# A decoder layer on one core: the row maxima of three batch pairs are added in PSUM by TensorE instead of by VectorE on the way to SBUF

## The chip, the core and the metric

The kernel runs on one core of one Trainium2 chip. The metric is the device time of one execution in microseconds; lower is better. The kernel before has a median of 912.19 us over 3 runs (910.69 to 912.86). The chip's instruction engines are TensorE (PE in the profile), VectorE (DVE), ScalarE (ACT), GpSimd (POOL) and SyncE (SP), each with a queue of its own that it works off in order. SyncE only issues DMAs here.

## The reference

One decoder layer on x of shape 16 x 128 x 256 in float32:

```
x = layernorm(x + attention(x))        # 16 heads of 16, full softmax over 128 keys, output projection
x = layernorm(x + recurrence(x, ctx))  # a running state per channel, exponentials of k = x, values v = ctx
x = layernorm(x + experts(x))          # 8 experts, 256 -> 1024 -> 256 with gelu, softmax gates
```

For the change only the softmax of the attention matters:

```
scores = softmax(einsum('bhse,bhte->bhst', q, k) * scale, axis=-1)
att    = einsum('bhst,bhte->bhse', scores, v)
```

In the experts each takes the best 128 of 128 tokens, that is all of them, so every token passes through every expert with its gate as weight.

## The kernel before, in words

**Pairs.** The 16 batches are worked in 8 pairs (p = 0 to 7) of 256 tokens. For each pair there is a chain of steps: X (transpose), QK and V (projections), S_0 to S_3 (scores), M_0 to M_3 (row maxima and shift), E_0 to E_3 (exponentials), T_0 to T_3 (transposes of the probabilities), W_0 to W_3 (products with the values and their sums), ATT, WO, NORM1, Y1, XEXP, REC_0 to REC_3 (the recurrence), BACK, NORM2 and the router's steps R_TURN to R_BIAS. A step name stands for its parts on all engines: S on TensorE, M on VectorE, E on ScalarE, T and W on several.

**Units.** Each of the four units u of a pair holds 8 heads of one batch in two groups of 4 heads, 128 x 512 numbers each, so a pair has 8 groups (QUADS). Scores of a group stand in half-banks of PSUM (`score_banks`, L464, and `half`, L475). Pair 0's unit 1 uses the tensors up_ps and down_ps; pair 1's units 0 and 1 use a part of down_ps, which the experts' down products write later.

**Softmax, two ways** (`direct`, L381, true for p < DIRECT = 1). For pair 0, VectorE takes negated row maxima (L1246) and ScalarE reads the scores in PSUM head by head, 32 activations of 128 x 128 with the maximum as bias (L1022). For all other pairs VectorE takes the maxima (L1246), then adds them to the scores on the way into the SBUF tensor probs (the shift, L1255), and ScalarE takes exponentials there, 8 activations of 128 x 512 (L1028). `shifted` counts the shifts, `probs_ready` the exponentials, `max_ready` the maxima. The probabilities of pairs 0 and 1 are transposed by TensorE (L699) and copied by ScalarE (pt_hi, L1041) and VectorE (pt_lo, L1266); from pair 2 on they are split into p_hi (ScalarE, L1034) and p_lo (VectorE, L1261) and transposed by DMA. W is TensorE's L722 and L723 and VectorE's L1272 to L1276, which ends in att.

**Experts.** A visit n is one pass of an expert's weights; pair p joins at visit JOIN[p] = 0, 5, 9, ... for 8 visits, so one or two pairs are in work at a time. A visit has 4 units (one pair) or 8 (two pairs); U(n, u) is the up product (L629 to L631; L905 to L909 for the very first), D(n, u) the down product (L932 to L934). ScalarE applies gelu (h_all, L1087) and rounds to h_hi (L1078), VectorE takes the rest h_lo (L1167). Weights come by DMA as raw pieces, which ScalarE rounds to w_hi (L1100) and VectorE completes to w_lo (L1167; GpSimd, L1494, for the first ones). At the end of a visit VectorE adds the down products with their gates (acc, L1377).

**What sets the order.** `plan` (L57) makes one line of items: U(0,0), U(0,1), U(0,2), U(0,3), U(1,0), D(0,0), D(0,1), U(1,1), D(0,2), U(1,2), D(0,3), U(1,3), U(2,0), D(1,0), D(1,1), U(2,1), D(1,2), U(2,2), ... with the numbers 0, 1, 2, ... Each engine goes through this line. The tables EARLY (pairs 1 and 2) and STEADY (the others) say behind which item each step of a pair stands; in pair 2's part item 39 is U(5,1), 40 D(4,2), 49 U(5,6), 51 U(5,7), 54 D(5,5), 56 D(5,6), 57 U(6,2), 61 D(6,0). Pair 0's steps and some of pair 1 to 3 stand ahead of the line in lists per engine (FIRST_PE, FIRST_ACT, FIRST_DVE, FIRST_POOL, L1571 to L1581). Within an item ScalarE takes h_hi and gelu first, then the steps outside of BY_TABLE, the weight splits, and last the steps of BY_TABLE (E_0 to E_3, XEXP, R_GATE), which need another activation table than gelu (L1137 to L1160). VectorE takes acc, h_lo, the steps, then the weight splits. On SyncE nothing of the order is touched.

TensorE's D(0,0) waits for the weights and for h_lo alone:

```
pe.wait_ge(h_ready, unit + 1)
pairs = len(active(n))
if n == 1 and u == 0:
    pe.wait_ge(x2_biased, 1)
```

## Time and profile before

| | |
|---|---|
| median of 3 runs | 912.19 us |
| lowest, highest | 910.69, 912.86 us |
| profiled execution, its own time | 912.31 us |
| its span | 910.5 us |
| mean granted TensorE clock | 0.984 |
| busy: TensorE | 872.2 us (96%) |
| busy: VectorE | 586.0 us (64%) |
| busy: ScalarE | 579.8 us (64%) |
| busy: GpSimd | 80.7 us (9%) |
| chain that ended last | TensorE 76%, ScalarE 9%, VectorE 5% |

How to read it: the profile is of one execution. Busy time counts what an engine executes, not the waiting or the issue of DMAs. The times of a timeline row are its start and its length in microseconds; "x8" says that eight instructions in a row are merged; a bracket at the end is the idle time of the engine ahead of the row and what ended it. Instructions on one engine overlap a little, so a row's length divided by its count is slightly above the distance from one to the next. PEclk is the granted TensorE clock as a share of 2.4 GHz; 0.50 is 1.2 GHz.

### The profile page before, as it was taken

How to read it: one execution, taken by the hardware profiler on the slowest of the kernel's cores; microseconds unless marked ns; L12 is line 12 of the kernel's file. 1: busy time of each engine (PE TensorE's matmuls, PEld its weight loads, DVE VectorE, ACT ScalarE, POOL GpSimd, SP SyncE). 2: the span in 40 equal slices, each digit the busy share in tenths (PEclk: the TensorE clock that was granted, in tenths of full speed). 3: DMA queues.
4: the chain of work that ended last, by engine and by line, in shares of the span. 5: the costliest groups of instructions: out<-in, count | busy, mean ns of one | idle time of the engine just before them, and what ended most of it. 6: DMA issues, size and time to landing. Idle time of an engine off the chain costs nothing.

```text
span 910.5 us, 17548 instructions
## 1 busy us (share of the span) xinstructions
PE 872.2 (96%) x6507; PEld 794.6 (87%) x6507; DVE 586.0 (64%) x1197; ACT 579.8 (64%) x975; POOL 80.7 (9%) x116
## 2 busy tenths in 40 slices
PE   7898878989999999999999999999999999999997
PEld 7788777879998998988988898889988888999997
DVE  6889698767766567656566675655675564333574
ACT  7688677766666555766557465665557665444683
POOL 4220012001200012000120010100120000000000
PEclk8899889999999999999999999999999999999999
DMA  8469998998849653785539854496537855655340
GB/s 265 153 228 340 367 320 297 290 305 274 276 132 240 221 186 127 192 250 188 166 109 240 236 184 150 133 238 220 175 125 194 246 187 163 193 187 176 96 139 12
DMA packets 196787, 187.09 MB, mean 205 GB/s; under 512 B 62024, under 2 KB 162144, under 8 KB 196704
## 3 DMA queue, kind: packets, MB, share of 16 engines
q1 hardware_dynamic: 196704, 185.98, 67.5%
q8 instruction: 53, 0.87, 0.4%
q14 instruction: 30, 0.25, 0.1%
HBM read 136.91 MB, written 36.44 MB: 190 GB/s over the span
## 4 chain that ended last, share of the span: by engine, by line
PE 76%; ACT 9%; DVE 5%; DMA 2%; issue 2%; SPq 1%; POOL 1%; POOLq 0%; ACTq 0%; DVEq 0%
PE down_ps L932 12%; PE down_ps L933 11%; PE down_ps L934 11%; PE up_ps L629 11%; PE up_ps L631 11%; PE up_ps L630 11%; DMA pt_lo<-p_lo 2%; ACT h_all L1087 2%; ACT probs L1028 1%; PE bank L651 1%; PE bank L676 1%; ACT L1087 1%; PE bank L629 1%; PE bank L630 1%; PE bank L631 1%
## 5 line engine op out<-in xcount | busy, mean ns | idle before, releaser
L1087 ACT ACTIVATE h_all<-up_ps,b_all 128x512 f32<-128x512 f32 (+1 forms) x296 | 182.2, 630 | 256.0 <-PE up_ps L631 245.4
L932 PE MATMUL down_ps<-w_hi,h_hi 128*128 128x256 f32 x1024 | 295.0, 288 | 4.4 <-DVE acc L1377 4.4
L1167 DVE TENSOR_TENSOR h_lo<-h_all,h_hi 128x512 fp32r<-128x512 f32 x256 | 176.0, 690 | 188.7 <-ACT h_hi L1078 188.0
L933 PE MATMUL down_ps<-w_lo,h_hi 128*128 128x256 f32 x1024 | 290.4, 284 | 0.0
L934 PE MATMUL down_ps<-w_hi,h_lo 128*128 128x256 f32 x1024 | 290.3, 283 | 0.0
L629 PE MATMUL up_ps<-x2t_hi,w_hi 128*128 128x512 f32 (+1 forms) x588 | 220.5, 375 | 2.7 <-DVE w_lo L1167 1.2
L631 PE MATMUL up_ps<-x2t_hi,w_lo 128*128 128x512 f32 (+1 forms) x588 | 215.7, 367 | 0.0
L630 PE MATMUL up_ps<-x2t_lo,w_hi 128*128 128x512 f32 (+1 forms) x588 | 215.0, 366 | 0.0
L932 PEld LDWEIGHTS down_ps<-w_hi,h_hi 128*128 128x128 f32 x1024 | 195.6, 191 | 13.0 <-issue 2.9
L933 PEld LDWEIGHTS down_ps<-w_lo,h_hi 128*128 128x128 f32 x1024 | 196.4, 192 | 7.0
L934 PEld LDWEIGHTS down_ps<-w_hi,h_lo 128*128 128x128 f32 x1024 | 196.4, 192 | 0.0
L1078 ACT ACTIVATE h_hi<-h_all 128x512 fp32r<-128x512 f32 x256 | 161.4, 631 | 33.5 <-PE down_ps L934 29.2
L631 PEld LDWEIGHTS up_ps<-x2t_hi,w_lo 128*128 128x128 f32 x588 | 111.3, 189 | 18.6
L629 PEld LDWEIGHTS up_ps<-x2t_hi,w_hi 128*128 128x128 f32 x588 | 112.4, 191 | 16.2 <-DVE w_lo L1167 1.4
L630 PEld LDWEIGHTS up_ps<-x2t_lo,w_hi 128*128 128x128 f32 x588 | 112.6, 191 | 10.5
L1167 DVE TENSOR_TENSOR w_lo<-w_raw,w_hi 128x512 fp32r<-128x512 f32 x89 | 60.9, 689 | 26.8 <-ACT w_hi L1100 26.8
L1461 POOL TENSOR_TENSOR var_eps<-moments,eps_row 128x2 f32<-128x2 f32 x24 | 7.9, 329 | 782.5 <-DVE moments L1177 782.5
L1100 ACT ACTIVATE w_hi<-w_raw 128x512 fp32r<-128x512 f32 x96 | 59.4, 628 | 0.0
L1377 DVE SCALAR_TENSOR_TENSOR acc<-down_ps,gate,acc 128x256 f32<-128x256 f32 x112 | 46.9, 475 | 3.1 <-PE down_ps L934 3.1
L1261 DVE TENSOR_TENSOR p_lo<-probs,p_hi 128x1024 f16<-128x1024 f32 x24 | 29.4, 1224 | 25.7 <-ACT p_hi L1034 25.7
L1246 DVE TENSOR_REDUCE neg_max<-bank 128x4 f32<-128x512 f32 x60 | 38.4, 680 | 4.8 <-PE bank L676 4.7
L1087 ACT ACT_TABLE_LOAD x27 | 34.6, 1283 | 0.5
(251 smaller groups left out, 948.8 us busy)
## 6 DMA issues: line engine op xcount, KB each, us to landing
w_hi<-w_parts SPq DMA_DIRECT2D x200, 256.0 KB, 3.3
w_lo<-w_parts SPq DMA_DIRECT2D x200, 256.0 KB, 3.6
w_raw<-in_w_dram SPq DMA_DIRECT2D x96, 256.0 KB, 4.3
w_parts<-w_hi SPq DMA_DIRECT2D x64, 256.0 KB, 4.1
w_parts<-w_lo SPq DMA_DIRECT2D x64, 256.0 KB, 4.6
x_in<-in_x_dram SPq DMA_DIRECT2D x8, 256.0 KB, 4.2
ctx_sb<-in_ctx_dram SPq DMA_DIRECT2D x8, 256.0 KB, 4.4
out_dram<-acc SPq DMA_DIRECT2D x8, 256.0 KB, 2.2
```

Source lines behind the costliest of these rows:

```text
L629: nc.tensor.matmul(ps, hi, rhs_hi, start=first, stop=False)
L630: nc.tensor.matmul(ps, hi, rhs_lo, start=False, stop=False)
L631: return nc.tensor.matmul(ps, lo, rhs_hi, start=False, stop=last)
L932: nc.tensor.matmul(ps, hi, w2h[:, c, :], start=c == 0 and j == 0, stop=False, skip_group_check=True)
L933: nc.tensor.matmul(ps, hi, w2l[:, c, :], start=False, stop=False, skip_group_check=True)
L934: mm = nc.tensor.matmul(ps, lo, w2h[:, c, :], start=False, stop=c == FC - 1 and j == PAIR - 1, skip_group_check=True)
L1078: nc.scalar.activation(h_hi[:, unit % HALF, :], h_all[:, unit % HALL, :], ACT.Copy).then_inc(h_hi_ready, 1)
L1087: a = nc.scalar.activation(h_all[:, unit % HALL, k * wide:(k + 1) * wide], up_ps[unit % 2][:, k * wide:(k + 1) * wide], ACT.Gelu_apprx_tan ...
L1100: nc.scalar.activation(piece((w1_hi, w2_hi)[i], i, q), raw(m, i), ACT.Copy)\
L1167: return nc.vector.tensor_tensor(dst, src, hi.bitcast(F32), ALU.subtract)
L1246: nc.vector.tensor_reduce(neg_max[:, g, :].rearrange("p (b a) -> p b a", b=2), by_tile_head(score_banks(p, u)[i], half(p, u)), AX_X, ALU.m ...
L1377: nc.vector.scalar_tensor_tensor(out=acc[:, p % 2, t, :], in0=by_tile(down_ps[down_banks(n)[a]])[:, t, :], scalar=gate[:, p % 3, t, n % E: ...
```

## The change

DIRECT becomes 3: pairs 0, 1 and 2 take the direct way, and that way is new. TensorE adds the negated maxima to the scores in PSUM: a product of the identity (a rounded copy, ident_r, made once by ScalarE) with neg_max repeated 128 times per head, two products of 256 columns for each group, 16 for each pair (`level`). ScalarE then takes one exponential of 128 x 512 for each group out of PSUM, without a bias. The 16 shifts of pairs 1 and 2 on VectorE fall away. The steps LEVEL_0 to LEVEL_2 get places on TensorE; pair 0's lists are reordered; pair 2's W_0 and W_1 move from items 54 and 55 to 56 and 57; D(0,0) gets a wait for pair 1's first four exponentials; waits on `shifted` become waits on `probs_ready` for these pairs. The scores of a second half-bank no longer start with a cleared bank. Pairs 3 to 7 stay as they are.

```diff
+        ident_r = sb("ident_r", [P, P], F32R)
...
-        neg_max = sb("neg_max", [P, QUADS, HQ])
+        neg_max = sb("neg_max", [P, QUADS, HQ], F32R)
...
+        def level_units(p, s):
+
+            if first(p):
+                return ((0,), (1,), (2, 3))[s - LEVEL_0]
+            return ((0, 1), (), (2, 3))[s - LEVEL_0]
+
+        def levelled(p, u, i):
+
+            if first(p) and u < 2:
+                return 2 * u + i + 1
+            return 4 * (u // 2) + 2 * i + 2
...
                 if u == 2 and by_dma(p):
-                    pe.wait_ge(shifted, QUADS * (p - DIRECT) + 4)
+                    if direct(p):
+                        pe.wait_ge(probs_ready, QUADS * p + 4)
+                    else:
+                        pe.wait_ge(shifted, QUADS * (p - DIRECT) + 4)
...
-                                              kd[at, k, c, :, rows], start=last == 0, stop=last == 2)
+                                              kd[at, k, c, :, rows], start=last == 0 and not (direct(p) and half(p, u)),
+                                              stop=last == 2, skip_group_check=direct(p))
...
+            def level(p, s):
+
+                taken = level_units(p, s)
+                for i in range(2):
+                    for u in taken:
+                        g = 2 * u + i
+                        pe.wait_ge(max_ready, QUADS * p + 2 * taken[-1] + i + 1)
+                        for b in range(2):
+                            mm = nc.tensor.matmul(by_tile_head(score_banks(p, u)[i], half(p, u))[:, b], ident_r[:],
+                                                  neg_max[:, g, 2 * b:2 * b + 2].rearrange("p (a o) -> p a o", o=1).to_broadcast([P, 2, S]),
+                                                  start=False, stop=True, skip_group_check=True)
+                        mm.then_inc(level_ps, 1)
...
                 if by_dma(p):
-                    if u == 0:
+                    if u == 0 and direct(p):
+                        pe.wait_ge(probs_ready, QUADS * (p + 1))
+                    if u == 0 and not direct(p):
                         pe.wait_ge(shifted, QUADS * (p - DIRECT + 1))
...
                 pairs = len(active(n))
+                if n == 0 and u == 0:
+                    pe.wait_ge(probs_ready, QUADS + 4)
...
             pe.wait_ge(masks_made, MASKS)
+            pe.wait_ge(ident_ready, 1)
...
                             g = 2 * u + i
-                            act.wait_ge(max_ready, QUADS * p + g + (1 if u % 2 or first(p) and u == 0 else 3))
-                            if u >= 2:
+                            act.wait_ge(level_ps, QUADS * p + levelled(p, u, i))
+                            if u >= 2 and by_dma(p):
+                                act.wait_ge(p_lo_ready, turns(p) + u - 1)
+                            if u >= 2 and not by_dma(p):
                                 act.wait_ge(pt_ps, QUADS * p + (g - 3))
-                            for h in range(HQ):
-                                a = nc.scalar.activation(probs[:, u % 2, i, h, :], by_tile_head(score_banks(p, u)[i], half(p, u))[:, h // 2, h % 2],
-                                                         ACT.Exp, bias=neg_max[:, g, h:h + 1])
-                            a.then_inc(probs_ready, 1)
+                            nc.scalar.activation(probs[:, u % 2, i].rearrange("p (b a) t -> p b a t", b=2),
+                                                 by_tile_head(score_banks(p, u)[i], half(p, u)), ACT.Exp).then_inc(probs_ready, 1)
...
+            act.wait_ge(masks_made, 4)
+            nc.scalar.activation(ident_r[:], ident[:], ACT.Copy).then_inc(ident_ready, 1)
             split_projection(PROJECTIONS[0])
...
-    {E_0: 3, E_1: 3, X_BIAS: 6, T_0: 7, T_1: 8, W_0: 10, W_1: 11, S_2: 13, M_2: 13, S_3: 13, M_3: 13, E_2: 15, E_3: 15, T_2: 17, T_3: 18, W_2: 20, W_3: 21,
+    {LEVEL_0: 1, E_0: 3, E_1: 3, X_BIAS: 6, T_0: 7, T_1: 8, W_0: 10, W_1: 11, S_2: 13, M_2: 13, S_3: 13, M_3: 13, LEVEL_2: 14, E_2: 15, E_3: 15, T_2: 17, T_3: 18, W_2: 20, W_3: 21,
...
-     S_0: 38, M_0: 38, S_1: 38, M_1: 38, DIAG_1: 40, E_0: 41, E_1: 41, T_0: 43, T_1: 45, S_2: 49, M_2: 49, S_3: 49, M_3: 50, W_0: 54, E_2: 54, E_3: 54, W_1: 55, T_2: 56,
+     S_0: 38, M_0: 38, S_1: 38, M_1: 38, LEVEL_0: 39, DIAG_1: 40, E_0: 41, E_1: 41, T_0: 43, T_1: 45, S_2: 49, M_2: 49, S_3: 49, M_3: 50, LEVEL_2: 51, E_2: 54, E_3: 54, W_0: 56, W_1: 57, T_2: 56,
...
-FIRST_PE = ([(0, s) for s in (X, QK, V, S_0, S_1, S_2, S_3, T_0, T_1, W_0, T_2, W_1, T_3, W_2)]
+FIRST_PE = ([(0, s) for s in (X, QK, V, S_0, S_1, LEVEL_0, LEVEL_1, S_2, S_3, T_0, T_1, LEVEL_2, W_0, W_1, T_2, T_3, W_2)]
...
-FIRST_ACT = ([(0, s) for s in (K_COPY, V, E_0, E_1, T_0, E_2, T_1, E_3, T_2, T_3)]
+FIRST_ACT = ([(0, s) for s in (K_COPY, V, E_0, E_1, T_0, T_1, E_2, E_3, T_2, T_3)]
...
-DIRECT = 1
+DIRECT = 3
```

## Rows read from the trace of the kernel before

**Rows 1.** Busy time of the engines in three stages (stretch, length, engines, PEclk, DMA share, GB/s).

```profile
16.00:33.00 17.00, 12.47 (x132) 11.19 (x132) 11.85 (x26) 13.61 (x41) 9.28 (x9) 0.70 0.64 196
...
82.00:105.00 23.00, 17.62 (x181) 16.71 (x182) 20.34 (x39) 16.45 (x31) 0.00 (x0) 0.95 1.05 368
...
190.00:910.00 720.00, 710.58 (x5170) 645.32 (x5168) 431.45 (x883) 437.82 (x692) 48.50 (x70) 1.00 0.63 185
```

**Rows 2.** Instructions that write or read probs (duration ns min/median/max, first and last start).

```profile
L1028 ACT ACTIVATE probs<-probs x56: 612/615/633, 64.3 to 706.5; 128x512 f32<-128x512 f32 x56
L1255 DVE TENSOR_TENSOR probs<-bank,neg_max x54: 675/678/682, 55.5 to 701.6; 128x512 f32<-128x512 f32 x54
```

**Rows 3.** Timeline of ScalarE, pair 0's exponentials and what follows them (start us, us).

```profile
15.40 2.09 ACT L1022 ACTIVATE probs<-bank,neg_max 128x128 f32<-128x128 f32 x8
...
19.40 1.13 ACT L1100 ACTIVATE w_hi<-w_raw 128x512 fp32r<-128x512 f32 x2
...
27.00 1.23 ACT L1041 ACTIVATE pt_hi<-up_ps 128x512 f16<-128x512 f32 x2
```

**Rows 4.** Timeline of TensorE, pair 0: S_2, T_0 and ATT.

```profile
17.63 0.80 PE L676 MATMUL bank<-kd,q_hi 32*128 32x256 f32 x8 [2.87 <-ACT probs L1022]
...
19.55 1.97 PE L699 MATMUL down_ps<-ident,probs 128*128 128x128 f32 x8 [0.26 <-ACT probs L1022]
...
33.31 0.66 PE L651 MATMUL bank<-ident,att 128*128 128x128 f32 x4 [0.17 <-DVE att L1276]
```

**Rows 5.** Timeline of TensorE: first product of U(1,0), first two of D(0,0).

```profile
61.99 0.38 PE L629 MATMUL up_ps<-x2t_hi,w_hi 128*128 128x256 f32 x1 [1.18 <-DVE w_lo L1167]
...
63.50 0.28 PE L932 MATMUL down_ps<-w_hi,h_hi 128*128 128x256 f32 x1
63.62 0.28 PE L933 MATMUL down_ps<-w_lo,h_hi 128*128 128x256 f32 x1
```

**Rows 6.** Timeline of ScalarE: pair 1's E_0 and E_1 and what follows.

```profile
64.33 2.18 ACT L1028 ACTIVATE probs<-probs 128x512 f32<-128x512 f32 x4
66.41 0.62 ACT L1078 ACTIVATE h_hi<-h_all 128x512 fp32r<-128x512 f32 x1
```

**Rows 7.** Timeline of TensorE: pair 1's S_2, U(2,1) and ATT.

```profile
82.49 0.51 PE L676 MATMUL bank<-kd,q_hi 32*128 32x256 f32 x8 [1.37 <-DVE att L1276]
...
84.93 0.28 PE L629 MATMUL up_ps<-x2t_hi,w_hi 128*128 128x256 f32 x1
...
104.76 1.12 PE L651 MATMUL bank<-ident,att 128*128 128x128 f32 x4 [4.00 <-DVE att L1276]
```

**Rows 8.** Waits of TensorE over the whole span (total us, times, longest us).

```profile
PE down_ps L864 <- ACT gate_t L1071: 1.0, 1, 1.0
```

**Rows 9.** Timeline of VectorE: pair 1's M_2 with its shifts, and pt_lo of T_2.

```profile
84.67 1.28 DVE L1246 TENSOR_REDUCE neg_max<-bank 128x4 f32<-128x512 f32 x2
85.87 1.28 DVE L1255 TENSOR_TENSOR probs<-bank,neg_max 128x512 f32<-128x512 f32 x2
...
95.12 1.29 DVE L1266 TENSOR_TENSOR pt_lo<-bank,pt_hi 128x512 f16<-128x512 f32 x2 [1.87 <-ACT pt_hi L1041]
```

**Rows 10.** Busy time behind the wait for pair 1's ATT (columns as in rows 1).

```profile
106.00:108.00 2.00, 2.00 (x11) 2.00 (x10) 0.77 (x2) 1.63 (x3) 0.00 (x0) 0.50 1.07 395
...
110.00:112.00 2.00, 2.00 (x19) 2.00 (x18) 1.04 (x3) 1.73 (x4) 0.00 (x0) 1.00 1.08 375
```

**Rows 11.** Timeline of TensorE in pair 2's part: D(4,2) and D(6,0).

```profile
146.73 0.28 PE L932 MATMUL down_ps<-w_hi,h_hi 128*128 128x256 f32 x1
...
186.21 0.36 PE L932 MATMUL down_ps<-w_hi,h_hi 128*128 128x256 f32 x1 [2.02 <-DVE acc L1377]
```

**Rows 12.** Timeline of VectorE in pair 2's part: M_1 and W_0.

```profile
147.77 1.28 DVE L1246 TENSOR_REDUCE neg_max<-bank 128x4 f32<-128x512 f32 x2
...
174.46 0.58 DVE L1272 TENSOR_REDUCE pv_sum<-bank 128x136 f32<-128x408 f32 x1
```

**Rows 13.** Timeline of ScalarE: pair 2's E_2 and E_3.

```profile
175.13 2.19 ACT L1028 ACTIVATE probs<-probs 128x512 f32<-128x512 f32 x4
```

More of the change, by code:

```diff
@@ L305, in decoder_layer @@
         max_ready = sem("max_ready")
+        ident_ready = sem("ident_ready")
+        level_ps = sem("level_ps")
         shifted = sem("shifted")
@@ L764, in attend @@
                     go_ahead(p, s)
+                if s in (LEVEL_0, LEVEL_1, LEVEL_2):
+                    level(p, s)
                 if s == X:
@@ L851, in route @@
                 if part == 4:
-                    if second(b):
+                    if second(b) and direct(b + 1):
+                        pe.wait_ge(probs_ready, QUADS * (b + 1) + 4)
+                    if second(b) and not direct(b + 1):
                         pe.wait_ge(shifted, QUADS * (b + 1 - DIRECT) + 4)
@@ L1256, in attend @@
                                                     by_tile_head(score_banks(p, u)[i], half(p, u)),
-                                                    neg_max[:, g, :].rearrange("p (b a o) -> p b a o", b=2, o=1).to_broadcast([P, 2, 2, S]),
+                                                    neg_max[:, g, :].bitcast(F32).rearrange("p (b a o) -> p b a o", b=2, o=1).to_broadcast([P, 2, 2, S]),
                                                     ALU.add).then_inc(shifted, 1)
@@ L1534 @@
  ATT, CTX, WO, NORM1, Y1, XEXP, REC_0, REC_1, REC_2, REC_3, BACK, NORM2,
- R_TURN, R_LOGITS, R_MAX, R_GATE, R_GATE_T, R_BIAS, K_LOW_1, Q_LOW_1, HEAD_X, HEAD_K_0, HEAD_K, HEAD_Q, HEAD_V) = range(58)
+ R_TURN, R_LOGITS, R_MAX, R_GATE, R_GATE_T, R_BIAS, K_LOW_1, Q_LOW_1, HEAD_X, HEAD_K_0, HEAD_K, HEAD_Q, HEAD_V, LEVEL_0, LEVEL_1, LEVEL_2) = range(61)
 DIAGONAL = (DIAG_0, DIAG_1)
```

## The prediction, made before any run of the changed kernel

> **What bounds the kernel now.** I read the stages first. From 190 us on, TensorE is busy 710.58 of 720 us; before that it is not: 12.47 of 17 us while pair 0's attention runs, 17.62 of 23 us in pair 1's second half [rows 1]. So up to 190 us a microsecond is set by the order of four in-order queues and can be won or lost; behind it TensorE alone counts, and nothing there can take a delay back. The change lies wholly in the first part: pair 0 at 14 to 33 us, pair 1 at 54 to 105, pair 2 at 145 to 190. The prices come from the group rows: a shift on VectorE lasts 0.68 us, an exponential of 512 columns 0.615 us [rows 2]. The timelines of those three places give the order, and I walk them step by step. Every wait of TensorE named below is the idle time in brackets at the end of its row. All sums are made against the profiled execution, 912.31 us (span 910.5); the median of the runs shown is 912.19, 0.12 less.
>
> **Pair 0: fewer, wider exponentials.** 32 exponentials of 128 columns become 8 of 512. The first sixteen run from 15.40 to 19.40, 0.25 us each in a row; the other sixteen stand at 22 and 25 us and end where pt_hi starts, at 27.00 [rows 3]. A wide one in a row takes 0.52: four stand between 64.33 and 66.41 [rows 6]. ScalarE so saves 16 x 0.25 - 4 x 0.52 = 1.9 us in each half. The Trainium skill, page "ScalarE: Activation LUTs", section "What ACT_TABLE_LOAD costs", prices an activation with a bias pointer at 280 ns + 0.833 ns per column, one without at 186 ns, with 93 ns of overlap; by that a half would save 2.6 us. The rows decide for 1.9.
> Against it stand the level products: TensorE may add only after VectorE's maximum (0.68 us each), and ScalarE reads only after that. In the first half the last maximum ends at 16.7, its products at about 17.15, the last exponential at 17.75 instead of 19.45. TensorE's S_2 starts at about 16.95 instead of 17.63 and T_0 at 18.35 instead of 19.55 [rows 4], since its array runs slowly there. T_0 and T_1 take 3.5 us, LEVEL_2 1.7 at that rate (8 x 0.21), so level 2 is in at 22.9 and 23.75 and the exponentials end at 25.45 instead of 27.2. VectorE, whose turn now comes without the 1.7 us gap before T_1, ends its last value sums at about 30.9 instead of 33.2, where ATT starts at 33.31 [rows 4]. From there everything up to 53 us hangs on that chain: **-2.3 us** (bounds -1.2, if the levels wait longer at the slow rate, and -4.0, the full 2 x 1.9, if the clock holds). The copy of the identity on ScalarE lies in 2.5 us in which ScalarE waits for the first weights: nothing; without that cover it costs one activation, 0.3.
>
> **Pair 1, first half: the new wait ahead of D(0,0).** LEVEL_0 goes behind U(0,1): 8 products of 256 columns. The nearest row is a product of 256 columns of the same type, one every 0.12 us (63.50, 63.62) [rows 5]: 1.0 us with the refill; at half rate it is 0.21, 1.7 us. I take 0.12. The maxima are ready by then, because four shifts less stand between them. U(0,2) and U(0,3) come 1.0 us later, but TensorE's wait of 1.18 us for w_lo at 61.99 [rows 5] goes, as VectorE reaches that split 2 us sooner. U(1,0) then ends at about 63.1, level with before.
> Now the wait that counts. D(0,0) starts at 63.50 [rows 5]. With the change it waits for pair 1's first four exponentials, because they read down_ps, which D(0,0) overwrites. Those stand in ScalarE's queue at item 3, behind two activations, a weight split, a table load and the router's exponential, and end at 66.41 [rows 6]; with U(0,3) late, at 67.1. TensorE stands from 63.1 to 67.2, **4.0 us**, and D(0,0), D(0,1), U(1,1), T_0 and all behind them stand with it. It had such a gap before ATT, at 104.76 [rows 7], and behind it the granted clock is 0.50, half of 2.4 GHz, at 106 to 108 us, and 1.00 only from 110 [rows 10]: 24 products cost 0.21 instead of 0.12, so 2.1 us more. (The Trainium skill, "TensorE: Matmul & The Clock Gate", section "Why this matters for your kernels", warns that a pause between bursts of matmuls brings the half rate back. The trace agrees with 0.50, and it speaks against this wait.) So TensorE is 3.7 + 2.1 = 5.8 late at U(1,1). It gets back what it used to wait: 1.0 for gate_t [rows 8], 1.37 for att at 82.49 [rows 7], and 0.8 in shorter gaps. VectorE's late value sums and D(1,0) both give S_2 at about 85.15: +2.65 us.
>
> **Pair 1, second half: LEVEL_2 holds U(2,1).** In the kernel before, U(2,1) starts at 84.93 straight behind D(1,1), while VectorE alternates maxima and shifts from 84.67 to 89.5 [rows 7, 9]. Now LEVEL_2 stands between them and waits for the third and fourth maximum. VectorE comes to M_2 at 87.5 (h_lo of the late U(2,0) first); four maxima of 0.6 end at 89.95, the products at 90.45, U(2,1) starts at 90.5: **+5.6 us**. Without any delay ahead it would still be 84.67 + 2.4 + 0.5 = 87.6, +2.7. Behind it hangs a closed chain: gelu of U(2,1), table load, four exponentials, h_hi, table load, gelu, T_2's pt_hi, and from 95.12 [rows 9] VectorE without a gap to att at 104.7. T_2 on TensorE now waits for all four exponentials, but ScalarE's queue is later than that. The 4 x 0.6 us that VectorE saves here end in the wait ahead of 95.12: they are worth nothing. Pair 1 in all: **+5.6**.
>
> **Pair 2.** LEVEL_0 stands behind U(5,1), where D(4,2) starts at 146.73 [rows 11]. The third and fourth maximum, at 147.77 before [rows 12], move to 146.57 and end at 147.25 and 147.8; products to 148.4: **+1.7**. The gate chain (gelu, table load, exponentials, h_hi, h_lo, acc) is ScalarE's, so VectorE's 2.4 us don't shorten it. LEVEL_2 behind U(5,7) finds its maxima nearly ready: +1.0. W_0 and W_1 move behind items 56 and 57, and W_0 now waits for all exponentials, 175.13 to 177.3 [rows 13], late by 1.0: 178.4. VectorE's two value sums, 1.1 us each, leave an empty stretch at 174.46 [rows 12] and stand now ahead of p_lo T_2 and T_3, and so ahead of acc, for which D(6,0) waits 2.02 us at 186.21 [rows 11]. By my walk acc comes at 188.6, D(6,0) at 188.8: **+2.6** with LEVEL_2's 1.0.
> DMA queues: no transfer is added. They are full at 82 to 105 us (share 1.05) [rows 1], so an earlier start gives them nothing to collide with that a later pair 1 would not relieve.
>
> **Sum.** -2.3 + 5.6 + 1.7 + 2.6 = +7.6: 912.31 + 7.6 = 919.9, less 0.12: **919.8 us**. The wide exponential from PSUM has no row: the same from SBUF lasts 0.615 [rows 2], two copies of 512 columns from PSUM 1.23 [rows 3]; both say the same, so 0.52 in a row stands, within 0.1 us over pair 1's eight. Lower end: pair 0 at -4.0, no slow clock (5.6 becomes 3.5), moved W at nothing (2.6 becomes 1.0): +2.2, 914.4. Upper end: pair 0 at -1.2, and the slow clock once more at D(6,0): 3.6 us of idle there against 2.0 before; 24 products, +2.1: 923.0.
>
> **Rivals.**
> (a) The clock holds at D(0,0), as it did over the 2.02 us at 186.21 [rows 11]: +5.5, 917.7. Against it: the clock behind 104.76 [rows 10].
> (b) The clock falls a second time at D(6,0): +9.7, 921.9. For it: idle nearer 4.0 than 2.0. Against: a walk through four queues tends to add up waits.
> (c) Only the level waits cost: D(0,0)'s 3.7 us vanish in the later waits of pair 1 and the moved W are free. -2.3 + 2.7 + 1.7 + 1.0 = +3.1, 915.3; with the clock held in pair 0 (-4.0), 913.5.
> (d) Faster: VectorE's queue sets the way to ATT, and each shift that goes shortens it. Place: the gapless stretch up to 104.7. It decides if U(2,1) starts no later than before, so that pt_lo T_2 is pulled forward by the 2.4 us. Then -2.3 - 2.4 + 1.9 (pair 2's 16 products at 0.12) = -2.8, 909.4. Against it: the 1.87 us in which VectorE waits for pt_hi ahead of 95.12 [rows 9].
>
> **Chances.** About 0.2% (1.8 us) either way can't be told from no change: 910.4 to 914.0. Forecast 0.35, (a) 0.15, (b) 0.15, (c) 0.20, of which 0.05 lies within 0.2%, (d) 0.15, of which 0.12 is faster and 0.03 within. Slower 0.35 + 0.15 + 0.15 + 0.15 = 0.80, same 0.08, faster 0.12. Range 913.5 to 923.5: it holds the forecast, (a), (b) and nearly all of (c), and leaves out (d).
>
> **What would show it.** Right: a wait of D(0,0) for probs of 3 to 4 us near 61 to 65 us (all is 2.3 earlier there) and a granted clock of 0.5 behind it; a wait of 1.5 to 2.5 us of the level products for neg_max before U(2,1); ATT of pair 0 near 31 and of pair 1 near 108; D(6,0) waiting 3 us or more for acc. Wrong: ATT of pair 1 before 104.8, or a stage behind pair 2 that is shorter or longer than its 720 us.

## Result and the profile after

The changed kernel takes 917.57 us (median of 5 executions, 913.14 to 918.40), the kernel before, run beside it, 912.32 (5, 910.69 to 914.82): ratio **1.0052**, 95% interval 1.0032 to 1.0072, slower by 4.7 us. The forecast was 919.8 in 913.5 to 923.5. The profiled execution is the lowest of the five, 913.14 us (span 911.4, mean granted clock 0.993); the other four took 917.55 to 918.40 at 0.985 to 0.988. So a second profile of the same kernel, of 915.63 us, is read beside it (the first experiment). That one too is the lowest of its round (the other five took 916.26 to 918.25); no profile shows an execution of the usual length.

Busy time of the changed kernel by stages, columns as in [rows 1]:

```profile
16.00:33.00 17.00, 14.11 (x167) 11.96 (x168) 15.53 (x31) 11.64 (x23) 9.92 (x10) 1.00 0.60 194
63.00:65.00 2.00, 1.98 (x10) 2.00 (x11) 0.69 (x1) 1.97 (x3) 0.00 (x0) 0.56 0.61 180
...
105.00:107.00 2.00, 1.21 (x11) 1.21 (x12) 1.27 (x4) 0.51 (x2) 0.00 (x0) 1.00 1.05 392
107.00:109.00 2.00, 2.00 (x20) 2.00 (x19) 1.38 (x2) 1.74 (x5) 0.00 (x0) 1.00 1.04 339
...
135.00:145.00 10.00, 7.92 (x72) 7.01 (x71) 8.25 (x18) 4.71 (x9) 5.54 (x4) 1.00 1.06 382
190.00:910.00 720.00, 712.20 (x5194) 646.81 (x5192) 432.67 (x885) 438.00 (x693) 48.53 (x70) 1.00 0.63 185
```

The clock no longer falls in pair 0 (0.70 before), it falls to 0.56 behind 63 us, and it does not fall at 105 to 109 us, where the kernel before has 0.50 [rows 10]. From 190 to 910 us TensorE is busy 712.20 us instead of 710.58 at a clock of 1.00: in this profile that part only lies later. Now TensorE's timeline, to be laid beside [rows 4, 5, 7, 11]:

```profile
15.90 0.51 PE L695 MATMUL bank<-kd,q_hi 32*128 32x256 f32 x8
...
29.27 0.66 PE L666 MATMUL bank<-ident,att 128*128 128x128 f32 x4 [0.28 <-DVE att L1320]
...
63.02 0.35 PE L973 MATMUL down_ps<-w_hi,h_hi 128*128 128x256 f32 x1 [3.97 <-ACT probs L1065]
...
80.99 0.51 PE L695 MATMUL bank<-kd,q_hi 32*128 32x256 f32 x8
...
84.93 1.31 PE L709 MATMUL bank<-neg_max,ident_r 128*128 128x256 f32 x8 [1.33 <-DVE neg_max L1290]
86.08 0.28 PE L644 MATMUL up_ps<-x2t_hi,w_hi 128*128 128x256 f32 x1
...
105.79 0.66 PE L666 MATMUL bank<-ident,att 128*128 128x128 f32 x4 [3.22 <-DVE att L1320]
...
147.31 0.28 PE L973 MATMUL down_ps<-w_hi,h_hi 128*128 128x256 f32 x1
...
187.77 0.35 PE L973 MATMUL down_ps<-w_hi,h_hi 128*128 128x256 f32 x1 [3.50 <-DVE acc L1421]
```

ATT of pair 0 comes at 29.27 instead of 33.31, and pair 1 turns these 4 us into a loss: D(0,0) waits 3.97 us for the exponentials, the level products 1.33 us for the maxima, and ATT of pair 1 is at 105.79 instead of 104.76. D(6,0) waits 3.50 us for acc instead of 2.02. Of the signs that the prediction named, the waits of D(0,0) and D(6,0) and the clock behind D(0,0) came as said. The level products wait 1.33 us ahead of U(2,1), a little under the 1.5 to 2.5 named; ATT of pair 0 is near 29 and not 31, ATT of pair 1 near 106 and not 108. ScalarE's and VectorE's rows of pair 1's second half, to be laid beside [rows 9]:

```profile
90.37 2.06 ACT L1065 ACTIVATE probs<-bank 128x512 f32<-128x512 f32 x4
```

```profile
83.00 2.48 DVE L1290 TENSOR_REDUCE neg_max<-bank 128x4 fp32r<-128x512 f32 x4
...
96.14 1.29 DVE L1310 TENSOR_TENSOR pt_lo<-bank,pt_hi 128x512 f16<-128x512 f32 x2 [1.86 <-ACT pt_hi L1083]
```

VectorE is done with the maxima at 85.5 and has no shifts, and waits 1.86 us ahead of pt_lo, as it did before (1.87). VectorE's rows ahead of D(6,0), to be laid beside [rows 12]: the first rows of the two value sums, then the addition that D(6,0) waits for.

```profile
181.16 0.58 DVE L1316 TENSOR_REDUCE pv_sum<-bank 128x136 f32<-128x408 f32 x1
...
183.96 0.58 DVE L1316 TENSOR_REDUCE pv_sum<-bank 128x136 f32<-128x408 f32 x1
...
186.75 0.87 DVE L1421 SCALAR_TENSOR_TENSOR acc<-down_ps,gate,acc 128x256 f32<-128x256 f32 x2
```

In the kernel before, the sums stood at 174.46 and 176.22, with 2.51 us of idle time of VectorE behind them. Now they stand among the splits that lead to acc, and VectorE has no gap from 179.95 to acc.

The table holds the steps of every profile as distances between starts of timeline rows (us), so that a shift in one part does not hide another. The last column names stretches of which the granted clock spent a good part at half: **p** 15 to 33 us (pair 0), **a** 61 to 69 us, **b** 100 to 111, **c** 131 to 146 (behind BACK of pair 1), **d** 171 to 195 (behind the waits of W_0 or D(6,0) in pair 2). Three more are left out of it: a fall at 120 to 135 us, behind the wait for mix, is in all but the last three rows (where it reaches past 131 us it is not counted as c); one at 92 to 98 us is in after_again, pairs01, w_back and fill_all; one at 153 to 162 us is in before, pair0, pair0_narrow, pair1_first and pairs01.

| kernel | S_0 to BACK, pair 0 | BACK 0 to S_2 of pair 1 | S_2 to ATT | ATT to BACK 1 | BACK 1 to S_0 of pair 2 | S_0 to S_2 | S_2 to end | half |
|---|---|---|---|---|---|---|---|---|
| before | 34.84 | 34.09 | 22.27 | 23.10 | 16.46 | 21.27 | 744.9 | p, b |
| after | 32.24 | 36.65 | 24.80 | 20.92 | 16.46 | 21.73 | 746.5 | a |
| after_again | 32.08 | 36.60 | 24.77 | 20.89 | 18.60 | 21.71 | 747.4 | a, c, d |
| pair0 | 33.05 | 34.09 | 22.28 | 22.45 | 16.46 | 21.27 | 744.5 | p, b |
| pair0_narrow | 32.15 | 34.09 | 22.28 | 23.61 | 16.45 | 21.25 | 744.6 | b |
| pair1_first | 32.62 | 36.58 | 22.29 | 22.44 | 16.45 | 21.26 | 743.4 | a, b |
| pairs01 | 32.66 | 36.36 | 24.78 | 20.90 | 18.60 | 21.27 | 744.3 | a, c |
| level_late | 31.63 | 37.76 | 22.14 | 23.50 | 16.46 | 21.72 | 747.7 | a, b, d |
| down_first | 32.15 | 35.62 | 24.77 | 23.51 | 16.46 | 21.73 | 746.7 | a, b, d |
| fill_wait | 32.80 | 35.03 | 24.79 | 23.61 | 16.46 | 21.73 | 747.2 | b, d |
| w_back | 32.91 | 36.63 | 24.79 | 20.92 | 18.60 | 21.73 | 747.2 | p, a, c, d |
| fill_all | 33.80 | 35.04 | 26.16 | 20.86 | 16.45 | 21.71 | 749.7 | p, d |
| pair0_fill | 32.15 | 34.10 | 22.27 | 20.93 | 18.82 | 20.14 | 744.0 | c |
| all_mended | 32.33 | 34.54 | 22.14 | 20.90 | 16.46 | 21.71 | 748.7 | d |

### The profile page after: what moved, and what is told of

Same layout as the page of the kernel before. It is cut to its first block, busy times and chain, and to the rows that moved or that the text cites. A ratio compares the mean times of both kernels' runs of the same rounds, so it can differ in the third digit from the quotient of the medians.

```text
span 911.4 us, 17605 instructions
## 1 busy us (share of the span) xinstructions
PE 871.3 (96%) x6555; PEld 792.7 (87%) x6555; DVE 578.2 (63%) x1181; ACT 576.0 (63%) x952; POOL 82.3 (9%) x116
## 4 chain that ended last, share of the span: by engine, by line
PE 76%; ACT 8%; DVE 7%; issue 2%; DMA 2%; SPq 1%; POOL 1%; POOLq 0%; ACTq 0%; DVEq 0%
PE down_ps L973 12%; PE down_ps L974 11%; PE down_ps L975 11%; PE up_ps L644 11%; PE up_ps L646 11%; PE up_ps L645 11%; DMA pt_lo<-p_lo 2%; ACT h_all L1129 1%; PE bank L666 1%; PE bank L695 1%; DVE w_lo L1211 1%; ACT L1129 1%; PE bank L646 1%; PE bank L644 1%; PE bank L645 1%
## 5 line engine op out<-in xcount | busy, mean ns | idle before, releaser
L645 PEld LDWEIGHTS up_ps<-x2t_lo,w_hi 128*128 128x128 f32 x588 | 111.8, 190 | 10.5
L1290 DVE TENSOR_REDUCE neg_max<-bank 128x4 fp32r<-128x512 f32 x60 | 38.3, 682 | 2.4 <-PE bank L695 2.3
```

Source lines behind the costliest of these rows:

```text
L645: nc.tensor.matmul(ps, hi, rhs_lo, start=False, stop=False)
L1290: nc.vector.tensor_reduce(neg_max[:, g, :].rearrange("p (b a) -> p b a", b=2), by_tile_head(score_banks(p, u)[i], half(p, u)), AX_X, ALU.m ...
```

## Experiments

**The same kernel once more.** No edit.

> The changed kernel as it is, profiled once more and timed again. The first profile of it was of its quickest execution: 913.14 us against 917.55 to 918.40 in the other four, mean granted clock 0.993 against 0.985 to 0.988. Theory A: the 4.4 us between them are a fall of the clock in pair 0's head (16 to 33 us), as the kernel before has it (0.70 over 16:33) and the first profile of after has not. Then a profile of a usual execution shows a clock of about 0.7 between 16 and 31 us, its BACK of pair 0 at 46 to 48.5 instead of 44.34, and the same steps after it. Theory B (rival): the clock falls somewhere else, behind D(0,0)'s wait (63 to 70 us) for longer or behind pair 1's ATT (105 to 112 us, 1.00 in the first profile, 0.50 in the kernel before). Then BACK of pair 0 stands at 44.3 again and the loss shows after 63 us. If the quick execution comes again, this run says only how often it comes: the median of the rounds should be 917 to 918.5.

Measured: 916.75 us, ratio 1.0059 (1.0046 to 1.0072); the profiled execution took 915.63 us (span 913.9). Its windows:

```profile
16.00:33.00 17.00, 14.23 (x167) 12.09 (x164) 15.84 (x32) 11.38 (x22) 11.11 (x11) 1.00 0.65 206
63.00:65.00 2.00, 2.00 (x11) 2.00 (x11) 0.66 (x1) 1.99 (x4) 0.00 (x0) 0.50 0.82 236
...
135.00:145.00 10.00, 8.65 (x43) 8.20 (x46) 6.86 (x15) 3.77 (x8) 4.92 (x4) 0.66 1.06 378
```

Theory A falls: pair 0's clock is whole again. The loss stands at 135 to 145 us (0.66 against 1.00 in the first profile), between BACK of pair 1 and S_0 of pair 2: 18.60 us instead of 16.46. Theory B named other places; it was right only in that the fall lies later.

There is one more: behind D(6,0) the clock is 1.00 in the first profile and 0.50 in the second, although D(6,0) waits 3.50 us for acc in both. First after, then after_again:

```profile
189.00:192.00 3.00, 3.00 (x36) 2.82 (x35) 2.53 (x6) 0.63 (x1) 0.00 (x0) 1.00 1.18 310
```

```profile
189.00:192.00 3.00, 2.65 (x12) 2.68 (x13) 2.79 (x6) 0.00 (x0) 0.00 (x0) 0.50 1.04 273
```

S_0 of pair 2 to the end takes 769.1 us instead of 768.2, 0.9 more. Of the six profiles with this wait of about 3.5 us, five show the fall (after_again, level_late, down_first, fill_wait and fill_all), and only the first profile of after does not.

**Pair by pair.** The three kernels differ in which halves of which pairs are levelled; all waits and counts follow the set, and pair 2's W_0 and W_1 stay at items 54 and 55 where it isn't levelled.

```diff
-            return p < DIRECT
+            return (p, u // 2) in LEVELLED
...
-DIRECT = 3
+LEVELLED = ((0, 0), (0, 1))
```

> Only pair 0 is levelled by TensorE; pairs 1 and 2 have VectorE's shift again (pair 2 with its value products where they were). My theory: pair 0 gains 2.3 us (1.2 to 4.0, the 4.0 if its clock holds) and everything slow comes from pairs 1 and 2: 908.3 to 911.1, most likely 910.0, and D(0,0) waits for nothing at 59 us. Rival 1: nothing is gained in pair 0 in a usual execution, and the first profile's 4.06 us there were a luck of the clock: 911.8 to 912.8. Rival 2: the loss is in pair 0 too, by the identity's copy and the 16 products of the first levels: above 913.

Measured: **908.28 us, ratio 0.9962 (0.9947 to 0.9977)**: pair 0 alone gains 3.5 us. S_0 to BACK takes 33.05 instead of 34.84, with a clock of 0.90 over 16 to 33 us where after has 1.00.

With ((0, 0), (0, 1), (1, 0)):

> Pair 0 and of pair 1 only the first two units (the half with D(0,0)'s new wait) are levelled by TensorE; the last two units of pair 1 and pair 2 have VectorE's shift. My theory: D(0,0) still waits 4.0 us for the exponentials at 59 to 63 us and the clock falls to half behind it, but without the level of the second half the loss is 2.9 us over the kernel with pair 0 alone (S_2 late by 2.65), and the second half's level wait has the other 2.7 of pair 1's 5.6. Rival 1: the first half costs all of pair 1's loss (the level wait at 83 to 85 us fills a gap that would be there anyway): within 1 us of the run with pairs 0 and 1. Rival 2: the late S_2 is taken up ahead of ATT, and the first half costs under 1 us.

Measured: 909.43 us, ratio 0.9984 (0.9974 to 0.9995), 2.0 us over pair0 by the ratios (1.15 by the medians). D(0,0) waits 3.97 us and S_2 of pair 1 is 2.49 us later behind BACK, as my theory has it; the cost at the end is less than its 2.9. The steps behind S_2 are as in pair0 up to S_2 of pair 2, and the part behind that is 1.1 us shorter (743.4 against 744.5).

With ((0, 0), (0, 1), (1, 0), (1, 1)):

> Pairs 0 and 1 are levelled by TensorE, pair 2 has VectorE's shift again with its value products where they were. My theory: pair 1 costs 5.6 us (4.0 to 6.0) over the kernel with pair 0 alone: 914.5 to 916.0. Pair 2 then has the remaining 2.0 to 3.0 of the whole. Rival: pair 2 costs most by its moved value products and its two level waits, and pair 1 under 3 us because its late attention is taken up by the wait for VectorE's mix at 127 us: below 913.

Measured: 913.85 us, ratio 1.0023 (1.0012 to 1.0035): pair 1 costs 5.6 us over pair0, in its second half 3.6 (4.4 by the medians). S_2 to ATT is 24.78 instead of 22.29. The median lies below the 914.5 to 916.0 of my theory, because pair0 came out lower than it had assumed; the cost over pair0 is as it said. Pair 2's share is the rest: 1.0059 - 1.0023, 3.3 us. The four shares, by the ratios: -3.5, +2.0, +3.6, +3.3. Each ratio's interval is 1.0 to 1.4 us wide to either side, so a single share can be off by more than 1 us.

**What pair 0's gain is made of.** pair0 with each exponential cut into four of 128 columns, without a bias:

```diff
+                            for h in range(HQ):
+                                a = nc.scalar.activation(probs[:, u % 2, i, h, :], by_tile_head(score_banks(p, u)[i], half(p, u))[:, h // 2, h % 2],
+                                                         ACT.Exp)
+                            a.then_inc(probs_ready, 1)
```

> The kernel with pair 0 alone levelled, but each of its exponential calls is cut into four of 128 columns again, without a bias: 32 short ones in place of 8 long ones, as many as the kernel before has. The levels and all else stay. Theory A (pair 0's gain is the shorter calls: 0.5 us of ScalarE where four took 1.0, so S_2 no longer waits 2.9 us and the clock no longer falls behind it): S_2 stands at 17.0 to 18.0 us again behind a wait of 2.5 to 3.5 us, the clock falls to about 0.7 over 16 to 30 us, BACK of pair 0 comes at 47.5 to 49.0 instead of 44.9, and the whole gain of 3.3 us is gone, the levels' own time with it: 911.5 to 913.5. Rival B (the gain is the exponentials' freedom from the bias and the order of levels, not the number of calls): under 1 us lost, 908 to 909.5. Rival C (calls cost 1.9 us a half but the clock holds): BACK at 46.5 to 47.5, 910 to 911.

Measured: 907.64 us, ratio 0.9951 (0.9939 to 0.9963). Nothing is lost; theory A falls, and rival B is the nearest, its 908 to 909.5 a little high. ScalarE's timeline of pair 0, first pair0, then this kernel ([rows 3] has before):

```profile
14.25 1.04 ACT L1075 ACTIVATE probs<-bank 128x512 f32<-128x512 f32 x2
15.21 0.57 ACT L1075 ACTIVATE probs<-up_ps 128x512 f32<-128x512 f32 x1
15.69 0.60 ACT L1075 ACTIVATE probs<-down_ps 128x512 f32<-128x512 f32 x1
```

```profile
14.70 1.47 ACT L1076 ACTIVATE probs<-bank 128x128 f32<-128x128 f32 x8 [0.17 <-PE bank L719]
15.97 0.88 ACT L1076 ACTIVATE probs<-up_ps 128x128 f32<-128x128 f32 x4
16.60 0.93 ACT L1076 ACTIVATE probs<-down_ps 128x128 f32<-128x128 f32 x4
17.22 1.33 ACT L1154 ACTIVATE w_hi<-w_raw 128x512 fp32r<-128x512 f32 x2
```

Sixteen short calls took 4.00 us with a bias, 2.52 (14.70 to 17.22) without, and four long ones 1.94 (14.25 to 16.19). So in the first half 1.48 of the 2.06 us come from the missing bias, 0.093 a call, and only 0.58 from the number of calls. That 0.58 is off the path: T_2 starts 9.94 us behind S_0 here and 9.97 in pair0. (The Trainium skill, "ScalarE: Activation LUTs", "What ACT_TABLE_LOAD costs", puts a bias pointer at about 93 ns a call; by that, the trace of the first half agrees.) In the second half the 16 calls take 3.02 us, 0.19 each, where those with a bias took 4.00 (22.05 to 24.05 and 25.00 to 27.00): there the bias is worth 0.061 a call. What this run doesn't part is the missing bias from the new order of pair 0's lists and from the clock, which is whole here (1.00 over 16 to 33 us, 0.70 in before); a kernel with the new order and the old bias was not tried.

**Pair 1's second level behind U(2,1).**

```diff
-    {... M_3: 13, LEVEL_2: 14, E_2: 15 ...
+    {... M_3: 13, LEVEL_2: 15, E_2: 15 ...
```

> All three pairs levelled; only pair 1's second level is issued behind U(2,1) instead of ahead of it. Taken from the kernel with pair 1's second half shifted again, that half costs 4.4 us of the median (913.85 against 909.43); in the traces its exponentials start 9.38 us behind S_2 instead of 6.73. Theory A (LEVEL_2's wait for the maxima holds U(2,1), and with it the gelu and the table load ahead of the exponentials): with U(2,1) ahead, the exponentials start 6.7 to 7.3 us behind S_2 again, ATT comes 2 to 2.6 us earlier, and the median falls to 913.5 to 915.0. Rival B (it is the exponentials' or the transposes' own order that is late, whoever holds U(2,1)): no more than 0.5 us gained, 916.2 to 917.5. Rival C: the attention is earlier, but then TensorE waits 4 us ahead of ATT and mix again and the clock falls behind it, which gives the gain back: ATT 2 us earlier, the end under 1 us.

Measured: 914.68 us, ratio 1.0032 (1.0022 to 1.0042), 2.5 us less than after_again. Beside 80.99 and 90.37 of after, S_2 and the exponentials:

```profile
81.47 0.51 PE L695 MATMUL bank<-kd,q_hi 32*128 32x256 f32 x8
```

```profile
88.20 2.06 ACT L1065 ACTIVATE probs<-bank 128x512 f32<-128x512 f32 x4
```

6.73 us apart instead of 9.38, and S_2 to ATT is 22.14: the hold of U(2,1) is the whole of that step. The saved shifts are worth 22.29 - 22.14 = 0.15 us. Behind BACK of pair 0, ATT comes 1.5 us earlier (59.90 instead of 61.37 in after_again) and not 2.5, since BACK to S_2 takes 1.2 longer here: the clock is slow until 69 us, in after_again until 66. Rival C is seen too: the clock is at 0.50 over 105 to 109 and ATT to BACK takes 23.50 instead of 20.9, but the fall at 135 to 145 is gone for it.

**D(0,0)'s wait filled with products.** 14 x 128 x 512 on a bank nobody reads:

```diff
                 if n == 0 and u == 0:
+                    idle_products(bank[1], 14)
                     pe.wait_ge(probs_ready, QUADS + 4)
```

> All three pairs levelled; 14 products of 128 x 512 whose results nobody reads are put ahead of D(0,0)'s wait, about 3.1 of its 4.0 us. D(0,0) starts no earlier; only TensorE is not idle before it. Theory A (the granted clock of 0.50 to 0.58 over 63 to 67 us comes from the idle time, and costs 2 us of pair 1): the clock is 1.0 over 63 to 70, S_2 of pair 1 comes 1.5 to 2.1 us earlier (34.5 to 35.1 us behind BACK of pair 0 instead of 36.6), median 914.5 to 915.5. Rival B: the clock falls all the same (the idle time is not what it goes by, or it falls later): no gain, 916.5 to 918. Rival C: the clock holds, but S_2 then waits for the attention's VectorE work as in the kernel before (1.37 us) and half of the gain is lost: 915.5 to 916.5.

Measured: 916.05 us, ratio 1.0043 (1.0033 to 1.0055). The wait is 0.65 us, and the windows read:

```profile
63.00:67.00 4.00, 3.75 (x31) 3.75 (x32) 1.27 (x2) 3.97 (x8) 0.00 (x0) 1.00 0.67 213
...
105.00:109.00 4.00, 4.00 (x21) 4.00 (x20) 1.46 (x3) 1.71 (x3) 0.00 (x0) 0.50 1.04 351
```

S_2 comes 35.03 us behind BACK, 1.6 earlier, as theory A says; but the end is only 0.7 us (medians) to 1.5 us (ratios) below after_again, and the intervals overlap. A fall now stands at 105 to 109 us (ATT to BACK 23.61), and of the three expectations none has this; C has its size, not its mechanism. That the filling brings this fall is not shown: level_late and down_first have it too, with the fall at 63 us still there.

**The exponentials on D(0,0)'s banks first.** In pair 1's first half, E_0 takes both groups in down_ps and E_1 the others; D(0,0) waits for the first two:

```diff
-                        for i in range(2):
-                            g = 2 * u + i
+                        for a, i in ([(0, 1 - u), (1, 1 - u)] if second(p) and u < 2 else [(u, 0), (u, 1)]):
+                            g = 2 * a + i
...
-                    pe.wait_ge(probs_ready, QUADS + 4)
+                    pe.wait_ge(probs_ready, QUADS + 2)
```

> All three pairs levelled; of pair 1's first four exponentials the two on the banks that D(0,0) writes come first, and D(0,0) waits for those two alone. Theory A (D(0,0) waits for ScalarE's exponentials in that bank and nothing else): D(0,0) starts 0.96 us earlier, its wait is 3.0 us instead of 3.97. If the clock still falls behind it: S_2 of pair 1 about 1 us earlier, median 915.5 to 916.5. If the shorter wait keeps the clock: 3 us earlier, 913.5 to 914.5. Rival B: D(0,0) waits for something else that ends at 63 us (h_hi or a weight): no change, 916.3 to 917.5.

Measured: 915.99 us, ratio 1.0048 (1.0034 to 1.0062).

```profile
61.72 0.36 PE L973 MATMUL down_ps<-w_hi,h_hi 128*128 128x256 f32 x1 [2.99 <-ACT probs L1065]
```

The wait is 2.99 instead of 3.97 us, S_2 1.0 us earlier, the clock still at 0.50 at 63 to 65: theory A's first branch for the steps. The end gains 0.8 us by the medians, which the intervals do not separate from after_again's, and a fall at 105 to 109 stands here too.

**Pair 2's value products back.**

```diff
-     ... LEVEL_2: 51, E_2: 54, E_3: 54, W_0: 56, W_1: 57, T_2: 56,
+     ... LEVEL_2: 51, W_0: 54, W_1: 55, E_2: 54, E_3: 54, T_2: 56,
```

> All three pairs levelled; pair 2's first two value products are back where they were, two items earlier. They wait for all exponentials of the pair now, not for the shift. Theory A (what my prediction said: the move costs, since the two value sums now stand ahead of the acc additions that D(6,0) waits for, 3.50 us instead of 2.02): D(6,0) waits about 2 us again and comes 1 to 1.5 us earlier; median 915.2 to 916.3. Rival B (the move saves: at the old place TensorE would stand at W_0 until the last exponential, at 177.4 us in the first profile of after, with U(6,1) behind it): W_0 waits 2 to 4 us, D(6,0) is no earlier, median 917 to 919.5.

Measured: 916.17 us, ratio 1.0046 (1.0033 to 1.0058); the intervals do not part it from after_again.

```profile
179.89 0.20 PE L757 MATMUL bank<-v_cat,pt_hi 128*128 128x51 bf16 x1 [3.43 <-issue]
...
191.03 0.36 PE L973 MATMUL down_ps<-w_hi,h_hi 128*128 128x256 f32 x1 [0.29 <-DVE acc L1421]
```

The median lies in theory A's range, but the steps are rival B's: W_0 waits 3.43 us, and D(6,0), whose wait is down to 0.29 us, stands 23.74 us behind S_2 of pair 2 against 22.87 in after and 20.62 before. The clock is 0.57 over 179 to 183 us, behind W_0's wait. W_0 stands at its new condition, pair 2's last exponential (177.72 + 2.06 = 179.78). At the old place W_0 holds TensorE until the last exponential; at the new one it waits only 0.61 us (in after), but its value sums stand ahead of acc. By the steps the move saves some 0.9 us, with one fall of the clock counted in w_back and none in after.

**All long waits of pair 1 filled.** fill_wait's products, and 14 ahead of ATT's and of BACK's wait:

```diff
+                    if second(p):
+                        idle_products(bank[3], 14)
                     pe.wait_ge(att_ready, UNITS * (p + 1))
...
+                    if second(p):
+                        idle_products(bank[1], 14)
                     pe.wait_ge(mix_ready, p + 1)
```

> All three pairs levelled; 14 products of 128 x 512 that nobody reads stand ahead of each of the three long waits of pair 1: D(0,0)'s for the exponentials, ATT's for the last value row, BACK's for the mix. With D(0,0)'s wait filled alone, ATT of pair 1 came 1.6 us earlier but the clock was at 0.50 over 105 to 109 us and BACK came no earlier. Theory A (each fall follows an idle stretch of TensorE of 3 to 4 us, and one that is prevented lets the next happen): with all three filled the clock is 1.0 from 58 to 145 us, BACK of pair 1 stands 79.5 to 81.5 us behind BACK of pair 0 instead of 82.3 to 83.9, S_0 of pair 2 16.5 behind it; median 912.0 to 914.5. Rival B (the falls go by something else, the load before them for one): a fall shows between 58 and 145 us all the same, median 915.5 to 917.5. Rival C: the fillers run into the waits' ends and delay what they fill: above 917.5.

Measured: 915.29 us, ratio 1.0044 (1.0029 to 1.0059). The falls at 63, 105, 120 and 135 us are gone, as theory A says:

```profile
105.00:109.00 4.00, 4.00 (x28) 3.60 (x27) 1.79 (x4) 1.38 (x3) 0.00 (x0) 1.00 0.94 331
...
120.00:131.00 11.00, 10.20 (x74) 9.27 (x73) 10.21 (x20) 9.13 (x20) 0.00 (x0) 1.00 1.01 343
...
135.00:145.00 10.00, 7.22 (x71) 6.57 (x70) 8.58 (x18) 5.12 (x10) 4.71 (x4) 1.00 1.06 383
```

One stays at 90 to 100 us (0.83), against theory A's clock of 1.0 throughout, and behind D(6,0)'s wait the clock is 0.50 to 0.52 over 189 to 195 us, longer than in the other kernels; S_2 of pair 2 to the end takes 749.7 us against 747.4 in after_again. BACK of pair 0 to S_0 of pair 2 is 98.51, 2.35 less than in after_again. But rival C is in it too: the products ahead of ATT run from 103.80 to 107.15 and ATT, at 106.98, comes 1.4 us later behind S_2. The median lies between, nearer to B's figure than to A's.

**The same on pair 0's kernel.** pair0 with the fillers ahead of ATT and BACK:

> The kernel with pair 0 alone levelled (908.28 us in its rounds), with the 14 products ahead of ATT's and of BACK's wait of pair 1. There its clock was 0.69 over 100 to 105, 0.93 over 105 to 107, 0.67 over 120 to 127 and 0.73 over 127 to 131 us. Theory A: these two falls go and give 1.0 to 1.8 us each: 904.5 to 907.0, ahead of both kernels by 0.6 to 0.8%. Rival B: a fall moves behind the fillers (145 to 168 us) or the fillers fall into it themselves: 907.5 to 909.5.

Measured: **906.17 us, ratio 0.9933 (0.9920 to 0.9946)**, the fastest kernel here, ahead of both. That is 2.6 us below pair0 by the ratios. The two falls that pair0 has are gone (1.00 over 100 to 109 and 120 to 131 us), and a new one stands at 0.60 over 131 to 135 and 0.82 to 145. A for the time, B for what the clock does. The steps of the profile don't put the gain where A has it: ATT to BACK is 1.5 us shorter (20.93), but the new fall gives back 2.4 (18.82 instead of 16.46), so BACK of pair 0 to S_0 of pair 2 takes 96.12, 0.8 more than in pair0. What is shorter stands elsewhere, 0.9 in pair 0 and 1.1 in S_0 to S_2 of pair 2, each where pair0 has a fall and this kernel none. And pair0_narrow, in the same rounds, has 907.64 us and an interval (0.9939 to 0.9963) that overlaps this one's. The five executions have a mean granted clock of 0.994 to 0.997, those of pair0 0.987 to 0.990, so fewer falls are not the luck of one profile; but which of them gives the time is not shown.

**All that helped, on three pairs.** level_late, down_first, w_back and the fillers (11 ahead of D(0,0)):

> All three pairs levelled, with what helped alone put together: pair 1's second level behind U(2,1), its exponentials on D(0,0)'s banks first, pair 2's value products back at their place, and the products ahead of the three waits of pair 1 (11 ahead of D(0,0)'s, which is shorter now). Theory A (levelling pairs 1 and 2 costs by where its waits fall, and most of that can be moved away; its products and VectorE's saved time are nearly free): 909 to 912, at or ahead of the kernel before, yet still behind pair 0 alone. Rival B (the single gains are the same gain and don't add up): 913 to 915. Rival C (with all waits moved away VectorE's saved 0.68 us a call pays, and pairs 1 and 2 gain): under 907.

Measured: 911.33 us, ratio 0.9992 (0.9982 to 1.0002): theory A. No fall from 58 to 168 us, and BACK of pair 0 to S_0 of pair 2 takes 94.04, 1.2 less than pair0. What is left is pair 2: S_0 of pair 2 to the end 770.4 us against 765.7 in pair0, all of it ahead of D(6,0) (46.70 us behind S_0, in pair0 41.88). There the next fall stands, behind W_0's wait of 3.44 us, and most of 171 to 179 us is at half clock:

```profile
168.00:190.00 22.00, 18.27 (x138) 15.73 (x137) 12.85 (x24) 14.76 (x22) 0.00 (x0) 0.84 0.89 231
```

In w_back, too, moving the value products back brought this wait and a later D(6,0). The same kernel without that move, or with products ahead of W_0's wait, was not tried; so it stays open what is left of pair 2's loss without this fall.

## Why the prediction was right, point by point

- **Pair 0, -2.3 (-1.2 to -4.0).** From S_0 to BACK the kernels with pair 0 levelled take 31.63 to 33.80, 34.84 before: a gain of 1.0 to 3.2 that holds the 2.3. Two steps of it did not hold. I took the clock as slow in T_0, T_1 and LEVEL_2; S_2 no longer waits 2.87 us [rows 4], and in ten of the thirteen profiles the stretch reads 1.00 instead of 0.70 [rows 1] (pair0, w_back and fill_all read 0.90 to 0.91). And I gave the 1.9 us a half to fewer calls, where 1.5 of the first half and 1.0 of the second are the bias (pair0_narrow). The median gain is larger, 3.5 us: every profile of a levelled kernel has S_0 of pair 0 at 11.70 to 12.61 us, before at 13.56, because its first products come 0.21 us apart until 10.5, those of pair0 0.12. There is one profile of before; whether its other executions start so was not seen. Whether the clock alone would gain in the kernel before, with S_2's wait filled, was not tried: the scores of units 0 and 1 stand in all eight PSUM banks there, so no bank is free for products that nobody reads.
  Two neighbouring products at the head of before, then of pair0:

```profile
8.12 0.41 PE L629 MATMUL bank<-xt_hi,proj_hi 128*128 128x256 f32 x1
8.33 0.41 PE L630 MATMUL bank<-xt_lo,proj_hi 128*128 128x256 f32 x1
```

```profile
8.44 0.28 PE L654 MATMUL down_ps<-xt_hi,proj_lo 128*128 128x256 f32 x1
8.56 0.28 PE L652 MATMUL down_ps<-xt_hi,proj_hi 128*128 128x256 f32 x1
```

- **Pair 1, first half.** The wait for probs was forecast at 4.0 and is 3.97; the clock behind it is 0.50 to 0.58 over 63 to 65 us, forecast at half; S_2 +2.65 forecast, +2.5 measured. At the end it costs 2.0.
- **Pair 1, second half.** LEVEL_2's own hold of U(2,1) was put at 2.7 and is 2.65 (U(2,1) stands 5.09 us behind S_2, 2.44 before), with 0.5 put for what follows the last maximum, which takes 0.6 (85.48 to 86.08); the exponentials come 2.65 later behind S_2, ATT 2.5. The saved shifts were put at nothing and are worth 0.15. Pair 1 in all: 5.6 forecast, 5.6 measured (pairs01 against pair0). That the two agree to 0.1 is in part luck: the two steps that I had give 2.3 + 2.5 = 4.8 in these profiles, and the clock falls of the next point add 0.6.
- **What I had not in the sum** is that the clock falls further on are not the same from kernel to kernel. With both waits of pair 1, ATT to BACK takes 20.9 instead of 23.1, 2.2 us back (against pair0 1.55; down_first, with a wait of 2.99 us, has 23.5), and in three of four such profiles (after_again, pairs01, w_back; not the first) 2.14 are lost again at 135 to 145 us. That is most of the difference between the first profile and the second. My rivals (a) and (b) had a fall more or less at the waits that I named, none moved. Rival (b)'s own fall, at D(6,0), is there in the second profile and in four other kernels with that wait; the forecast had given it no time. It cost 0.9 us in after_again where (b) put 2.1, and the forecast of one fall fits the first profile alone.
- **Pair 2, +1.7 and +2.6.** LEVEL_0 is right at its place: from S_0 to D(4,2) 4.14 us, before 2.41 [rows 11], +1.73. It is nearly all gone at S_2 (+0.46): before, pair0, pair0_narrow, pair1_first and pairs01 have a clock fall behind D(5,0) (0.73 over 158 to 163 in before), and after has none. D(6,0): +2.25 behind S_2 for the forecast 2.6, with a wait of 3.50 where I asked for 3 or more. Its two terms are in the rows: E_2 stands 10.43 us behind S_2, before 9.54 (LEVEL_2, +0.89 for 1.0), and acc 11.42 behind E_2, before 10.06 (+1.36 for 1.6), with the two value sums between them. So the reason that I gave, the moved sums ahead of acc, holds for the change as it is; w_back adds that putting them back is no cure, since W_0's new wait for the exponentials then holds TensorE. Together 2.7 in the profile, 3.3 by the ratios, for 4.3 forecast; what was over is mostly LEVEL_0's 1.7, of which 0.46 is left at S_2.
- **The sum** was +7.6, the ratios give +4.7 to +5.4. Over by 1.2 in pair 0 and 1.0 in pair 2; pair 1, which decides the sign, came out as forecast. The walk through the queues was right in its waits; which clock falls a given execution has was not foreseen, and that they came near to cancelling is luck. Rival (d) needed U(2,1) no later than before; level_late gives just that, and VectorE's shifts were still worth 0.15, not 2.4. (Rival (c)'s second time adds up to 913.6, not 913.5.)

## What to carry to other kernels

An addition moved from VectorE (PSUM to SBUF) to TensorE (inside PSUM) is not priced by the engine time saved: it changes who frees the bank, here the exponential in place of the shift, 3.4 to 4.0 us later where D(0,0) and, in w_back, W_0 wait for it, and puts a wait in TensorE's in-order queue ahead of work that had none. Here it paid only in pair 0, where ScalarE's calls lose their bias and no product waits for the new exponentials ahead of other work; so take the change apart by stage and keep the part that gains. And measure a fix to one stall by the end and in more than one profile, not by the step behind it: with the falls of pair 1 filled away, another stood further on, at 105 us in fill_wait, at 131 in pair0_fill, at 171 in all_mended and at 189 in fill_all.

## What was not expected of the hardware

- A per-partition bias on a 128-column exponential costs 0.093 us a call in a row (0.25 against 0.158) in the first half of pair 0, and 0.061 us (0.25 against 0.189) in the second.
- The same idle time ahead of the same step gives either clock. D(6,0) follows 3.50 us of idle in both profiles of the changed kernel, with a clock of 1.00 behind it (189 to 192) in one and 0.50 in the other. ATT of pair 1 follows 3.22 us of idle in after with 1.00 behind it (105 to 109), and 3.21 in fill_wait with 0.50. The 3.90 to 3.97 us ahead of D(0,0) were followed by about half in all kernels that have them, and the 2.99 of down_first too.
- With products that nobody reads ahead of a wait, the fall at that wait was gone in all four kernels that have them, and another one showed further on. Whether the one brings the other is not shown.
- The two profiled executions of the changed kernel differ by 2.5 us; 2.1 of that is whether one such fall happens, at 135 to 145 us, and 0.9 whether another does, at 189 to 192 us. Why they do in one and not in the other stays open.
- At the head of the kernel before, products of 256 columns come 0.21 us apart until 10.5 us, the distance of half clock, while the granted clock reads 1.00 there.
